# Windowed linear attention on one core: full out products of 144 columns with a selection behind them, k and v side by side, other orders at the ends

## The chip, the core and the metric

The kernel runs on one core of a Trainium2 chip, everything in fp32. The metric is the device time of one execution in microseconds, as a median over runs. TensorE (PE in the rows, its weight loads PEld) multiplies into PSUM; VectorE (DVE) and ScalarE (ACT) read PSUM; GpSimd (POOL) works in SBUF alone; SyncE (SP) issues the DMAs.

## The reference

`x` is 4 x 128 x 96 x 96. It is group-normalised (32 groups), cut into windows of 4 x 4 pixels and projected by a 1 x 1 convolution to q, k and v (16 heads of 8). A 5 x 5 average pool of q, k and v inside each window gives a second set of 16 heads. Each window and head gets linear attention, and both sets go through one more 1 x 1 convolution, a folded batch norm and the residual:

```
qkv = einsum('nchw,oc->nohw', xw, qkv_w); pooled = avg_pool5(qkv)
q, k, v = relu(msq[..., :8]), relu(msq[..., 8:16]), pad(msq[..., 16:], 1.0)
kv  = einsum('ngld,nglm->ngdm', k, v)
out = einsum('ngld,ngdm->nglm', q, kv)
out = out[..., :-1] / (out[..., -1:] + 1e-15)
y   = batch_norm(einsum('nchw,oc->nohw', out, proj_w));  return x + y
```

In a 4 x 4 window a 5 x 5 pool has only 9 different outputs, so the kernel carries 9 pooled pixels for each window and weights them.

## The kernel before

`x` is cut into 96 strips (`NS`) of 4 rows, 384 pixels or 24 windows each. All of `x` stays in SBUF (`x_all`). Each engine has its own instruction stream, written out by hand, and semaphores tie the streams together; nothing reorders them. TensorE's steps 1 to 94 are a hardware loop of two steps per pass; the other engines' streams are unrolled.

The names below end in `_f` or "full" for the 16 pixels of a window and in `_p` or "pooled" for the 9. TensorE's step `s` does, in this order:

- `conv_kv(s + 1)` (L587): k and v of the next strip, six products of 128 columns
- `transposes(s - 1)` (L695): the divided outputs turned back; waits for `kvc_f` of strip `s`
- `conv_kv_pooled(s + 1)` (L597)
- `project(s - 1)` (L704, L706): the output convolution; with `out_next` it first waits for `kvc_p` of strip `s`, since the out products that stand behind it need the masked tables
- `out_products(s)`, `out_products_pooled(s)` (L630): q times the table, 48 products of 72 columns each; the pooled ones wait for `added_f` and `y_copied`
- `kv_products(s + 1)` and its pooled twin (L615): k times v, 24 products of 144 columns and 16 of 216; the pooled ones write the PSUM banks 4 and 5 that the full out products also use, so they wait for `num_f`
- `conv_q(s + 1)` (L603, L604)

These products run as tiles of 64 rows x 32 columns of the array, eight in different places. A block of 32 rows holds two windows of 16 pixels. In a full out product of before each window of a block has its own product; its q stands in a `q_full` block padded with zeros for the other window, and the two accumulate in the same 72 columns.

VectorE's step `s`: `own_heads` for full and pooled (L509) copies the tables `kv` out of PSUM into `kvc_full` and `kvc_pool` with a mask, two instructions of 864 columns each, and gives `kvc_f` and `kvc_p`; then statistics of the next batch in some steps, `residual(s - 1)` (L515), and `divide` (L524, L525, L528) for full and pooled, which waits for `out_f` and `out_p`, reads PSUM and gives `num_f` and `num_p`.

ScalarE's step `s`: `relu_q`, `relu_q_pooled`, `relu_k`, `copy_v` of strip `s + 1`, `to_image` and `pooled_out` of strip `s - 1`, `relu_k_pooled`, then `masked_v_pooled`: six copies (L357, e = 0 to 5), with `copy_y_pooled` (L394) after the second. GpSimd normalises and pools the strip two ahead, then adds the pooled half of the residual. SP spreads `v_full` into `vm_full` by four DMAs a strip, loads later batches and stores.

Of the kernel before, what the change touches and what calls it, by code (L numbers as in the profile page):

```python
# [37 lines left out]
C_PACK = C_TP + EP  # L38
# [3 lines left out]
def constants():  # L42
# [14 lines left out]
    c[:, C_TP:C_TP + EP] = own_p * times  # L57
    pads = p % Q4 >= WP * PXP
# [4 lines left out]
def build(nc, x, wq, wkv, proj, bn, consts, out):  # L63
# [20 lines left out]
    with ExitStack() as ctx:  # L84
# [56 lines left out]
        KVF, OUTP, KVP, OUTF = 0, 2, 4, 4  # L141
        TRF, TRP = 0, 1
        Y_F, Y_P = 0, 1
        K_F, V_F = 2, 3
        K_P, V_P = 6, 7
        Q_F, Q_P = 6, 7
# [16 lines left out]
        projT_ready = sem("projT_ready")  # L163

        xn_ready, xp_ready = sem("xn_ready"), sem("xp_ready")
        k_f, v_f, k_p, v_p = sem("k_f"), sem("v_f"), sem("k_p"), sem("v_p")
# [8 lines left out]
        num_f, num_p = sem("num_f"), sem("num_p")  # L175
        tr_f, tr_p = sem("tr_f"), sem("tr_p")
# [17 lines left out]
        def over_strips(step):  # L194


            for s in range(NS):
                b, t = divmod(s - 3, SPB)
                at = t * 2 if s >= 3 and b + 1 < B and t < 2 * FOURS else None
                phase = t - 2 * FOURS if s >= 3 and b + 1 < B and 0 <= t - 2 * FOURS < 4 else None  # L200
                step(s, b + 1, at, phase)

# [50 lines left out]
        def _(pool):  # L253
            PL = 7
            pool.memset(xp[:], 0.0).then_inc(pads_zero, 1)
            pool.memset(q_full[:], 0.0).then_inc(pads_zero, 1)
# [7 lines left out]
            def normalise_and_pool(s, p):  # L264
# [11 lines left out]
                def link(ins, n):  # L276
                    ins.then_inc(pl, 1)
                    pool.wait_ge(pl, s * PL + n)
# [6 lines left out]
                rows = xd[:].rearrange("p (r g e c) -> p r g e c", r=WS, e=EF, c=WS)  # L285
                for r in range(WS):
# [10 lines left out]
                add(xo[:, :, :, 2, :], v3, h3[:, :, :, 3, :]).then_inc(pl, 1)  # L297
                add(xo[:, :, :, 1, :], xo[:, :, :, 0, :], h3[:, :, :, 3, :]).then_inc(xp_ready, 1)
# [23 lines left out]
            pool.wait_ge(pads_zero, 5)  # L322
            pool.wait_ge(dv_group, GS)
            normalise_and_pool(0, 0)
            normalise_and_pool(1, 1)
            over_strips(step)
            residual_pooled(NS - 1)

        @block.scalar
        def _(act):  # L330
            def relu_k(s):
                act.wait_ge(k_f, s + 1)
                wait(act, kv_f, s)
                act.activation(k_full[:].rearrange("p t c -> p (t c)"), ps[:, K_F, 0:TF * P],
                               ACT.Relu).then_inc(km_f, 1)

            def relu_k_pooled(s):
                act.wait_ge(k_p, s + 1)
                wait(act, kv_p, s)
                act.activation(k_pool[:].rearrange("p t c -> p (t c)"), ps[:, K_P, 0:TP * P],  # L340
                               ACT.Relu, scale=1 / 25.0).then_inc(km_p, 1)

            def copy_v(s):
                act.wait_ge(v_f, s + 1)
                wait(act, vm_f, 16 * EF * s)
                act.activation(v_full[:].rearrange("p t (h c) -> p t h c", c=HC)[:, :, :, 0:D],
                               ps[:, V_F, 0:TF * P].rearrange("p (t h m) -> p t h m", t=TF, m=D),
                               ACT.Copy).then_inc(v_copied, 1)

            def masked_v_pooled(s, between=None):  # L350

                act.wait_ge(v_p, s + 1)
                wait(act, kv_p, s)
                heads = vm_pool[:].rearrange("p e t (h c) -> p e t h c", c=HC)
                src = ps[:, V_P, 0:TP * P].rearrange("p (t h m) -> p t h m", t=TP, m=D)
                for e in range(EP):
                    last = act.activation(heads[:, e, :, :, 0:D], src, ACT.Copy, scale=col(C_VP + e))  # L357
                    if between is not None and e == 1:
                        copy_y_pooled(between)
                last.then_inc(vm_p, 1)  # L360

            def relu_q(s):


                act.wait_ge(q_f, s + 1)
                wait(act, out_f, s)
                act.activation(q_full[:].rearrange("p n e j -> p (n e) j").rearrange(  # L367
                                   "p (g w) j -> p g w j", w=EF)[:, :, :, 0:PX],
# [26 lines left out]

            def square_root(n):
# [6 lines left out]
            act.wait_ge(pads_zero, 5)  # L403

            def step(s, b, at, phase):
                relu_q(s)
                relu_q_pooled(s)
                if not is_last(s):
                    relu_k(s + 1)
                    copy_v(s + 1)  # L410
                if not is_first(s):
                    to_image(s - 1)
                    pooled_out(s - 1)
                if not is_last(s):
                    relu_k_pooled(s + 1)
                    masked_v_pooled(s + 1, None if is_first(s) else s - 1)
                elif not is_first(s):
                    copy_y_pooled(s - 1)
                if phase == 2:
                    square_root(b + 1)  # L420

            relu_k(0)
            copy_v(0)
            relu_k_pooled(0)
            masked_v_pooled(0)
            over_strips(step)
            to_image(NS - 1)
            pooled_out(NS - 1)
            copy_y_pooled(NS - 1)

        @block.vector
        def _(dve):
# [46 lines left out]

            dve.memset(mv[:], 0.0).then_inc(mv_zero, 1)  # L480
# [12 lines left out]
            group_rstd(0, 1)  # L493

# [22 lines left out]

            def divide(s, pooled):
                ready, done, turned, bank, tiles, den, o, step = (
                    (out_p, num_p, tr_p, OUTP, TP, den_pool, o_pool, 2) if pooled else  # L520
                    (out_f, num_f, tr_f, OUTF, TF, den_full, o_full, 0))
                dve.wait_ge(ready, s + 1)
                src = ps[:, bank:bank + G, 0:tiles * QG * KC].rearrange("p g (n c) -> p g n c", c=HC)
# [7 lines left out]
            def step(s, b, at, phase):  # L531
# [18 lines left out]
                elif phase == 3:  # L550
                    group_rstd(b, b + 2)
                if not is_first(s):
                    residual(s - 1)
                divide(s, False)
# [20 lines left out]
            residual(NS - 1)  # L575

        @block.tensor
        def _(pe):
            pe.wait_ge(loaded_w, 16 * 5)

            def conv_kv(s, p):
# [3 lines left out]
                for half, bank, done in ((0, K_F, k_f), (1, V_F, v_f)):  # L585
                    for t in range(TF):
                        last = pe.matmul(ps[:, bank, t * P:(t + 1) * P], xn[:, p, t * P:(t + 1) * P],  # L587
                                         wkv_sb[:, half * P:(half + 1) * P], start=True, stop=True)
                    last.then_inc(done, 1)

            def conv_kv_pooled(s, p):
# [3 lines left out]
                for half, bank, done in ((0, K_P, k_p), (1, V_P, v_p)):  # L595
                    for t in range(TP):
                        last = pe.matmul(ps[:, bank, t * P:(t + 1) * P], xp[:, p, t * P:(t + 1) * P],  # L597
# [176 lines left out]
```

## Time and profile before

| | |
|---|---|
| median of 3 runs | 895.9 us (895.72 to 898.23) |
| the profiled execution, its own time | 900.88 us |
| its span | 899.1 us |
| granted TensorE clock, mean | 0.993 |
| TensorE matmul busy | 859.1 us, 96% |
| VectorE / GpSimd / ScalarE busy | 77% / 74% / 57% |

The span runs from the first to the last instruction; the 1.8 us between it and the execution's own time lie around it. Busy shares are an average over the span. The engines' busy time doesn't say which of them the others wait for: that is read from the order of starts within a step.

### The profile page before, as it was taken

How to read it: one execution, taken by the hardware profiler on the slowest of the kernel's cores; microseconds unless marked ns; L12 is line 12 of the kernel's file. 1: busy time of each engine (PE TensorE's matmuls, PEld its weight loads, DVE VectorE, ACT ScalarE, POOL GpSimd, SP SyncE). 2: the span in 40 equal slices, each digit the busy share in tenths (PEclk: the TensorE clock that was granted, in tenths of full speed). 3: DMA queues.
4: the chain of work that ended last, by engine and by line, in shares of the span. 5: the costliest groups of instructions: out<-in, count | busy, mean ns of one | idle time of the engine just before them, and what ended most of it. 6: DMA issues, size and time to landing. Idle time of an engine off the chain costs nothing.

```text
span 899.1 us, 65691 instructions
## 1 busy us (share of the span) xinstructions
PE 859.1 (96%) x29282; PEld 740.6 (82%) x29282; DVE 695.4 (77%) x1236; ACT 509.9 (57%) x1350; POOL 666.7 (74%) x1641
## 2 busy tenths in 40 slices
PE   0789999999999999999999999999999999999996
PEld 0667888888888888888888888888888888888885
DVE  7466888888677888888776888888777777777775
ACT  0344656565655656565656556565656565565653
POOL 2666778777878777777878787777878787877772
PEclk9999999999999999999999999999999999999998
DMA  6122232111113232211113232211111111111111
GB/s 232 40 75 65 86 104 82 46 48 46 47 64 100 85 97 87 68 46 47 47 47 90 92 100 84 80 52 50 47 49 47 46 47 47 47 49 45 53 50 37
DMA packets 39082, 60.07 MB, mean 67 GB/s; under 512 B 8560, under 2 KB 33648, under 8 KB 39024
## 3 DMA queue, kind: packets, MB, share of 16 engines
q1 hardware_dynamic: 39024, 59.52, 19.7%
q14 instruction: 49, 0.40, 0.2%
q8 instruction: 9, 0.15, 0.1%
HBM read 19.38 MB, written 18.87 MB: 43 GB/s over the span
## 4 chain that ended last, share of the span: by engine, by line
PE 94%; DVE 2%; DMA 1%; issue 1%; SPq 0%; POOL 0%; ACT 0%; POOLq 0%; DVEq 0%
PE ps L630 23%; PE ps L615 17%; PE ps L587 15%; PE ps L597 9%; PE ps L603 9%; PE ps L704 7%; PE ps L695 6%; PE ps L706 4%; PE ps L604 4%; DVE stats L442 1%; DMA vm_full<-v_full 1%; DMA x_all<-x 1%; SPq L232 0%; DVE kvc_full L509 0%; POOL xn L287 0%
## 5 line engine op out<-in xcount | busy, mean ns | idle before, releaser
L357 ACT ACTIVATE vm_pool<-ps,cst 128x256 f32<-128x256 f32 x576 | 231.0, 481 | 5.1 <-PE ps L597 0.5
L367 ACT ACTIVATE q_full<-ps 128x384 f32<-128x384 f32 x96 | 47.3, 492 | 285.0 <-PE ps L603 285.0
L284 POOL TENSOR_TENSOR xd<-x_all,mean_t 128x384 f32<-128x384 f32 x96 | 79.5, 828 | 159.7 <-PE ps L604 143.0
L509 DVE TENSOR_TENSOR kvc_full<-ps,cst 128x864 f32<-128x864 f32 x192 | 193.2, 1048 | 5.2 <-PE ps L615 5.2
L509 DVE TENSOR_TENSOR kvc_pool<-ps,cst 128x864 f32<-128x864 f32 x192 | 193.1, 1047 | 1.4 <-PE ps L615 1.4
L587 PE MATMUL ps<-wkv_sb,xn 128*128 128x128 f32 x1152 | 146.4, 278 | 24.0 <-POOL xn L287 24.0
L587 PEld LDWEIGHTS ps<-wkv_sb,xn 128*128 128x128 f32 x1152 | 145.2, 194 | 24.0 <-issue 24.0
L262 POOL TENSOR_TENSOR x_all<-y_pool,x_all 128x96 f32<-128x96 f32 x384 | 150.8, 427 | 17.2 <-ACT y_pool L394 17.2
L287 POOL TENSOR_TENSOR xn<-xd,rstd_t 128x96 f32<-128x96 f32 x384 | 123.4, 369 | 7.5
L630 PEld LDWEIGHTS ps<-kvc_full,q_full 64*32 64x32 f32 x9216 | 108.0, 105 | 25.3 <-issue 25.2
L630 PE MATMUL ps<-kvc_full,q_full 64*32 64x72 f32 x9216 | 124.8, 230 | 0.0
L630 PE MATMUL ps<-kvc_pool,q_pool 64*32 64x72 f32 x9216 | 116.1, 231 | 2.9 <-issue 2.9
L515 DVE SCALAR_TENSOR_TENSOR x_all<-ps,shift,x_all 128x384 f32<-128x384 f32 x96 | 59.3, 618 | 71.2 <-PE ps L704 71.0
L630 PEld LDWEIGHTS ps<-kvc_pool,q_pool 64*32 64x32 f32 x9216 | 101.7, 105 | 3.7 <-issue 3.2
L597 PE MATMUL ps<-wkv_sb,xp 128*128 128x128 f32 x768 | 102.5, 277 | 0.7 <-POOL xp L262 0.7
L615 PE MATMUL ps<-vm_full,k_full 64*32 64x144 f32 x4608 | 95.6, 289 | 3.3 <-DMA vm_full<-v_full 3.3
L615 PE MATMUL ps<-vm_pool,k_pool 64*32 64x216 f32 x3072 | 96.0, 347 | 2.2 <-issue 2.2
L262 POOL TENSOR_TENSOR hs<-ht,xn 128x96 f32<-128x96 f32 x192 | 85.0, 443 | 15.0
L597 PEld LDWEIGHTS ps<-wkv_sb,xp 128*128 128x128 f32 x768 | 94.1, 193 | 1.0 <-POOL xp L262 1.0
L524 DVE TENSOR_SCALAR den_full<-ps 128x48 f32<-128x48 f32 x96 | 20.0, 208 | 92.2 <-PE ps L630 92.2
L603 PE MATMUL ps<-xn,wq_sb 128*128 128x384 f32 x192 | 88.8, 544 | 0.0
L704 PE MATMUL ps<-o_sb,projT 128*128 128x384 f32 x192 | 78.6, 491 | 0.7 <-ACT o_sb L382 0.7
(67 smaller groups left out, 1295.9 us busy)
## 6 DMA issues: line engine op xcount, KB each, us to landing
vm_full<-v_full SPq DMA_DIRECT2D x384, 54.0 KB, 1.9
out<-x_all SPq DMA_DIRECT2D x96, 192.0 KB, 1.9
x_all<-x SPq DMA_DIRECT2D x36, 384.0 KB, 3.5
x_all<-x SPq DMA_DIRECT2D x6, 768.0 KB, 8.1
cst<-consts SPq DMA_DIRECT2D x1, 170.0 KB, 11.0
wkv_sb<-wkv SPq DMA_DIRECT2D x1, 128.0 KB, 10.8
o_sb<-proj SPq DMA_DIRECT2D x1, 128.0 KB, 10.2
wq_sb<-wq SPq DMA_DIRECT2D x1, 64.0 KB, 10.5
```

The costliest lines, as they stand in the source:

```text
L262: return pool.tensor_tensor(o, a, b, ALU.add)
L284: link(pool.tensor_tensor(xd[:], x_all[:, s * SP:(s + 1) * SP], mean, ALU.subtract), 1)
L287: last = pool.tensor_tensor(xr[:, r], rows[:, r], rstd, ALU.mult)
L357: last = act.activation(heads[:, e, :, :, 0:D], src, ACT.Copy, scale=col(C_VP + e))
L509: last = dve.tensor_tensor(kvc[:, g], src.to_broadcast(shape), own, ALU.mult)
L515: dve.scalar_tensor_tensor(xs, ps[:, Y_F, 0:SP], shift[:], xs, ALU.add, ALU.add).then_inc(added_f, 1)
L587: last = pe.matmul(ps[:, bank, t * P:(t + 1) * P], xn[:, p, t * P:(t + 1) * P], wkv_sb[:, half * P:(half + 1) * P], start=True, stop=True)
L597: last = pe.matmul(ps[:, bank, t * P:(t + 1) * P], xp[:, p, t * P:(t + 1) * P], wkv_sb[:, half * P:(half + 1) * P], start=True, stop=True)
L603: pe.matmul(ps[:, Q_F, 0:SP], wq_sb[:], xn[:, p], start=True, stop=True).then_inc(q_f, 1)
L615: last = pe.matmul(ps[Q4 * i:Q4 * (i + 1), bank + r, t * n:(t + 1) * n], k[rows, t, Q4 * i:Q4 * (i + 1)], vm[rows, :, t, i * KC:(i + 1) * KC],
L630: last = pe.matmul(ps[Q4 * c:Q4 * (c + 1), bank + g, t * n:(t + 1) * n], blocks[rows, 4 * t + c, Q4 * e:Q4 * (e + 1)], kvc[rows, r, w], st ...
L704: pe.matmul(ps[:, Y_F, 0:SP], projT[:, 0:P], o_sb[:, 0:SP], start=True, stop=True).then_inc(y_f, 1)
```

## The change

Full out products: one product takes both windows of a block at once. Its stationary operand is the block's q without padding, its moving operand the tables of both windows, 144 columns, and it doesn't accumulate: 24 products in place of 48. Every row then has the results of both windows side by side, and only one is its own. `first_window` on ScalarE copies the results for window 0 of all rows to `sel_full` in SBUF (432 elements per partition); `copy_predicated` on VectorE then overwrites the rows of window 1. `divide` reads `sel_full`. Pooled out products stay as they were.

k and v: three (full) and two (pooled) products of 256 columns in place of six and four of 128, with one semaphore each (`conv_f`, `conv_p`). On ScalarE `copy_v` goes ahead of `relu_k`, and `relu_k` behind `pooled_out`. Strip 0 is normalised and pooled on VectorE; strip 1's k and v are made earlier; the last strip has another order and bank, and its pooled residual is VectorE's.

```diff
@@ bands and buffers
-        q_full = sb("q_full", [TF * 4, WF, Q4 + PX])
+        q_full = sb("q_full", [TF * 4, Q4])
+        sel_full = sb("sel_full", [G, TF, QG * KC])
-        K_F, V_F = 2, 3
-        K_P, V_P = 6, 7
-        Q_F, Q_P = 6, 7
+        KV_F, KV_P = 2, 6
+        Q_F, Q_P = 7, 6
@@ ScalarE
+            def first_window(s):
+                act.wait_ge(out_f, s + 1)
+                wait(act, num_f, s)
+                bank = OUTF_LAST if is_last(s) else OUTF
+                act.activation(sel_full[:], full_windows(bank)[:, :, :, 0], ACT.Copy).then_inc(win_f, 1)
...
                 for e in range(EP):
                     last = act.activation(heads[:, e, :, :, 0:D], src, ACT.Copy, scale=col(C_VP + e))
                     if between is not None and e == 1:
                         copy_y_pooled(between)
+                    if e == 3 and s > 0:
+                        first_window(s - 1)
@@ VectorE, divide, full
-                dve.wait_ge(ready, s + 1)
-                src = ps[:, bank:bank + G, 0:tiles * QG * KC].rearrange("p g (n c) -> p g n c", c=HC)
+                    dve.wait_ge(win_f, s + 1)
+                    own = col(C_WIN + 1).bitcast(mybir.dt.uint32).unsqueeze(2).unsqueeze(3)
+                    dve.copy_predicated(sel_full[:], own.to_broadcast([P, G, TF, QG * KC]),
+                                        full_windows(bank)[:, :, :, 1]).then_inc(sel_f, 1)
+                    dve.wait_ge(sel_f, s + 1)
+                    src = sel_full[:].rearrange("p g t (n c) -> p g (t n) c", c=HC)
@@ TensorE
+            def out_group_f(t, bank):
+                n = WF * QG * KC
                 for g in range(G):
                     rows = slice(H64 * g, H64 * (g + 1))
                     for c in range(4):
-                        r, w = c // QG, t * QG * wins + c % QG * wins + e
-                        last = pe.matmul(ps[Q4 * c:Q4 * (c + 1), bank + g, t * n:(t + 1) * n],
-                                         blocks[rows, 4 * t + c, Q4 * e:Q4 * (e + 1)], kvc[rows, r, w],
-                                         start=e == 0, stop=e == wins - 1)
+                        r, w = c // QG, (t * QG + c % QG) * WF
+                        last = pe.matmul(ps[Q4 * c:Q4 * (c + 1), bank + g, t * n:(t + 1) * n],
+                                         q_full[rows, 4 * t + c], kvc_full[rows, r, w:w + WF],
+                                         start=True, stop=True)
@@ kv_products_pooled
-                wait(pe, num_f, s)
+                wait(pe, sel_f, s)
```

VectorE, one step in the loop's steady part, before (each group ends with the tables of the next step; the word behind "waits" is the semaphore):

```order
L524 TENSOR_SCALAR den_full<-ps 128x48 [waits out_f]
L525 RECIPROCAL den_full<-den_full 128x48 [waits dv]
L528 TENSOR_TENSOR o_full<-ps,den_full 128x2x192 [waits tr_f,dv]
L524 TENSOR_SCALAR den_pool<-ps 128x32 [waits out_p]
L525 RECIPROCAL den_pool<-den_pool 128x32 [waits dv]
L528 TENSOR_TENSOR o_pool<-ps,den_pool 128x2x128 [waits tr_p,dv]
L509 TENSOR_TENSOR kvc_full<-ps,cst 128x864 [waits out_f,kv_f]
```

The same place after the change:

```order
L613 COPY_PREDICATED sel_full<-cst,ps 128x432 [waits win_f]
L617 TENSOR_SCALAR den_full<-sel_full 128x48 [waits sel_f]
L618 RECIPROCAL den_full<-den_full 128x48 [waits dv]
L621 TENSOR_TENSOR o_full<-sel_full,den_full 128x2x192 [waits tr_f,dv]
L617 TENSOR_SCALAR den_pool<-ps 128x32 [waits out_p]
L618 RECIPROCAL den_pool<-den_pool 128x32 [waits dv]
L621 TENSOR_TENSOR o_pool<-ps,den_pool 128x2x128 [waits tr_p,dv]
L577 TENSOR_TENSOR kvc_full<-ps,cst 128x864 [waits out_f,kv_f]
```

One instruction is new, and the first wait of the group is now for ScalarE's `win_f` and not for TensorE's `out_f`.

ScalarE, the same step, before:

```order
L340 ACTIVATE k_pool<-ps 128x256 [waits kv_p,k_p]
L357 ACTIVATE vm_pool<-ps,cst 128x32x8 [waits kv_p,v_p]
L357 ACTIVATE vm_pool<-ps,cst 128x32x8
L394 ACTIVATE y_pool<-ps 128x216 [waits y_done,y_p]
L357 ACTIVATE vm_pool<-ps,cst 128x32x8 x4
```

And after:

```order
L351 ACTIVATE k_full<-ps 128x384 [waits kv_f,conv_f]
L356 ACTIVATE k_pool<-ps 128x256 [waits kv_p,conv_p]
L373 ACTIVATE vm_pool<-ps,cst 128x32x8 [waits kv_p,conv_p]
L373 ACTIVATE vm_pool<-ps,cst 128x32x8
L411 ACTIVATE y_pool<-ps 128x216 [waits y_done,y_p]
L373 ACTIVATE vm_pool<-ps,cst 128x32x8 x2
L418 ACTIVATE sel_full<-ps 128x432 [waits num_f,out_f]
L373 ACTIVATE vm_pool<-ps,cst 128x32x8 x2
```

The window copy stands behind the fourth of the six `vm_pool` copies, and `k_full` has moved to the front of this piece.

## Rows read from the trace of the kernel before

**Rows 1.** The page: busy time by engine, and the chain that ended last.

```profile
PE 859.1 (96%) x29282; PEld 740.6 (82%) x29282; DVE 695.4 (77%) x1236; ACT 509.9 (57%) x1350; POOL 666.7 (74%) x1641
...
PE 94%; DVE 2%; DMA 1%; issue 1%; SPq 0%; POOL 0%; ACT 0%; POOLq 0%; DVEq 0%
```

**Rows 2.** Timeline of PE in one step: start us, length us, instruction, count.

```profile
234.38 0.81 PE L704 MATMUL ps<-o_sb,projT 128*128 128x384 f32 x2
235.02 0.53 PE L706 MATMUL ps<-o_sb,projT 128*128 128x216 f32 x2
235.48 1.30 PE L630 MATMUL ps<-kvc_full,q_full 64*32 64x72 f32 x96
236.57 1.20 PE L630 MATMUL ps<-kvc_pool,q_pool 64*32 64x72 f32 x96
237.66 0.98 PE L615 MATMUL ps<-vm_full,k_full 64*32 64x144 f32 x48
238.39 0.98 PE L615 MATMUL ps<-vm_pool,k_pool 64*32 64x216 f32 x32
...
240.41 1.50 PE L587 MATMUL ps<-wkv_sb,xn 128*128 128x128 f32 x12
241.75 0.49 PE L695 MATMUL ps<-cst,o_full 128*128 128x128 f32 x3
...
243.19 0.81 PE L704 MATMUL ps<-o_sb,projT 128*128 128x384 f32 x2
```

**Rows 3.** Timeline of DVE in the same step.

```profile
236.82 0.21 DVE L524 TENSOR_SCALAR den_full<-ps 128x48 f32<-128x48 f32 x1 [0.97 <-PE ps L630]
...
238.02 0.18 DVE L524 TENSOR_SCALAR den_pool<-ps 128x32 f32<-128x32 f32 x1
...
238.97 2.01 DVE L509 TENSOR_TENSOR kvc_full<-ps,cst 128x864 f32<-128x864 f32 x2
240.90 2.01 DVE L509 TENSOR_TENSOR kvc_pool<-ps,cst 128x864 f32<-128x864 f32 x2
```

**Rows 4.** Timeline of ACT in the same step.

```profile
235.59 0.35 ACT L394 ACTIVATE y_pool<-ps 128x216 f32<-128x216 f32 x1 [0.17 <-PE ps L706]
235.84 1.57 ACT L357 ACTIVATE vm_pool<-ps,cst 128x256 f32<-128x256 f32 x4
```

**Rows 5.** Timeline near the end, where PE does wait for other engines.

```profile
883.50 2.01 DVE L509 TENSOR_TENSOR kvc_full<-ps,cst 128x864 f32<-128x864 f32 x2
...
885.57 0.55 PE L695 MATMUL ps<-cst,o_full 128*128 128x128 f32 x3 [0.42 <-DVE kvc_full L509]
...
886.69 0.91 PE L704 MATMUL ps<-o_sb,projT 128*128 128x384 f32 x2 [0.36 <-ACT o_sb L382]
...
888.01 0.35 ACT L394 ACTIVATE y_pool<-ps 128x216 f32<-128x216 f32 x1 [1.12 <-PE ps L706]
```

**Rows 6.** Groups by line and shape: busy us, mean ns of one.

```profile
L509 DVE TENSOR_TENSOR kvc_full<-ps,cst 128x864 f32<-128x864 f32 x192 | 193.2, 1048 | 5.2 <-PE ps L615 5.2
L262 POOL TENSOR_TENSOR x_all<-y_pool,x_all 128x96 f32<-128x96 f32 x384 | 150.8, 427 | 17.2 <-ACT y_pool L394 17.2
...
L528 DVE TENSOR_TENSOR o_full<-ps,den_full 128x384 f32<-128x384 f32 x96 | 53.6, 559 | 3.3
...
L367 ACT ACTIVATE q_full<-ps 128x384 f32<-128x384 f32 x96 | 47.3, 492 | 285.0 <-PE ps L603 285.0
...
L375 ACT ACTIVATE q_pool<-ps 128x216 f32<-128x216 f32 x96 | 34.5, 360 | 0.2 <-PE ps L604 0.2
```

**Rows 7.** Timeline of PE in the first steps.

```profile
27.62 2.08 PE L597 MATMUL ps<-wkv_sb,xp 128*128 128x128 f32 x8 [0.72 <-POOL xp L262]
...
43.14 1.69 PE L615 MATMUL ps<-vm_full,k_full 64*32 64x144 f32 x48 [2.06 <-DMA vm_full<-v_full]
...
50.13 0.81 PE L704 MATMUL ps<-o_sb,projT 128*128 128x384 f32 x2
...
68.93 0.96 PE L615 MATMUL ps<-vm_pool,k_pool 64*32 64x216 f32 x30 [2.18 <-issue]
```

More of the change, by code:

```diff
@@ L37 @@
 C_TP = C_VP + EP
-C_PACK = C_TP + EP
+C_WIN = C_TP + EP
+C_PACK = C_WIN + WP
 N_CONST = C_PACK + P
@@ L407, in step @@
                 relu_q_pooled(s)
-                if not is_last(s):
-                    relu_k(s + 1)
+                if not is_first(s) and not is_last(s):
                     copy_v(s + 1)
@@ L413, in step @@
                     pooled_out(s - 1)
+                if not is_first(s) and not is_last(s):
+                    relu_k(s + 1)
                 if not is_last(s):
@@ L416, in step @@
                     masked_v_pooled(s + 1, None if is_first(s) else s - 1)
-                elif not is_first(s):
+                else:
                     copy_y_pooled(s - 1)
+                    first_window(s)
                 if phase == 2:
                     square_root(b + 1)
+            copy_v(0)
             relu_k(0)
-            copy_v(0)
             relu_k_pooled(0)
             masked_v_pooled(0)
+            copy_v(1)
+            relu_k(1)
             over_strips(step)
@@ L516, in residual, with residual_pooled_last @@
                                          ALU.add).then_inc(added_f, 1)
+            def residual_pooled_last():
+                s = NS - 1
+                dve.wait_ge(y_p, s + 1)
+                dve.wait_ge(added_f, s + 1)
+                dve.wait_ge(y_done, s)
+                src = ps[:, Y_P, 0:SPP].rearrange("p (w r c) -> p w r c", r=NP, c=NP)
+                dst = x_all[:, s * SP:(s + 1) * SP].rearrange("p (r w c) -> p w r c", r=WS, c=WS)
+                ends, ends_p, mid, mid_p = slice(0, WS, WS - 1), slice(0, NP, NP - 1), slice(1, 3), slice(1, 2)
+                for rows, rows_p in ((ends, ends_p), (mid, mid_p)):
+                    for cols, cols_p in ((ends, ends_p), (mid, mid_p)):
+                        part = dst[:, :, rows, cols]
+                        last = dve.tensor_tensor(part, src[:, :, rows_p, cols_p].to_broadcast([P, NW, 2, 2]), part,
+                                                 ALU.add)
+                last.then_inc(y_done, 1)
             def divide(s, pooled):
@@ L584, in conv_kv @@
                 wait(pe, num_p, s - 1)
[L585 to L589, printed above, removed]
+                for t in range(TF):
+                    bank, at = KV_F + t // 2, t % 2 * 2 * P
+                    last = pe.matmul(ps[:, bank, at:at + 2 * P], xn[:, p, t * P:(t + 1) * P], wkv_sb[:],
+                                     start=True, stop=True)
+                last.then_inc(conv_f, 1)
             def conv_kv_pooled(s, p):
@@ L594, in conv_kv_pooled @@
                 wait(pe, qm_p, s)
-                for half, bank, done in ((0, K_P, k_p), (1, V_P, v_p)):
-                    for t in range(TP):
-                        last = pe.matmul(ps[:, bank, t * P:(t + 1) * P], xp[:, p, t * P:(t + 1) * P],
-                                         wkv_sb[:, half * P:(half + 1) * P], start=True, stop=True)
-                    last.then_inc(done, 1)
+                for t in range(TP):
+                    last = pe.matmul(ps[:, KV_P, t * 2 * P:(t + 1) * 2 * P], xp[:, p, t * P:(t + 1) * P], wkv_sb[:],
+                                     start=True, stop=True)
+                last.then_inc(conv_p, 1)
             def conv_q(s, p):
@@ L618, in kv_tile @@
                 return last
-            def out_tile(pooled, t, e):
-                q, kvc, bank, wins = (q_pool, kvc_pool, OUTP, WP) if pooled else (q_full, kvc_full, OUTF, WF)
-                n = QG * KC
-                blocks = q[:].rearrange("p n e j -> p n (e j)")
+            def out_group_f(t, bank):
+                n = WF * QG * KC
                 for g in range(G):
@@ L654, in out_wait @@
                     pe.wait_ge(qm_p, s + 1)
-                pe.wait_ge(kvc_p, s + 1)
+                    pe.wait_ge(kvc_f, s + 1)
+                else:
+                    pe.wait_ge(kvc_p, s + 1)
             def out_products(s):
@@ L663, in out_products @@
                 for t in range(TF):
-                    for e in range(WF):
-                        last = out_tile(False, t, e)
+                    last = out_group_f(t, OUTF_LAST if is_last(s) else OUTF)
                 last.then_inc(out_f, 1)
```

129 lines of the change are left out of this document (102 added, 27 removed).

## The prediction

> **What bounds the kernel now.** I read the page first, then the timelines of TensorE, VectorE and ScalarE side by side over one step in the steady part, then the two ends. The page says TensorE: its matmuls are busy 96% of the span and the chain that ended last runs 94% through it [rows 1]. In the step no matmul group starts late; from one `project` to the next, 234.38 to 243.19, is 8.81 us [rows 2]. So a shorter TensorE stream would pay, as long as nobody else becomes late.
>
> The page can't say how close the next one is. For that I follow VectorE from the end of the full out products. `den_full` starts at 236.82, 2.44 us after `project`; VectorE then never pauses until both `own_heads` are done: den_full at 236.82, den_pool at 238.02, kvc_full at 238.97, kvc_pool at 240.90 and 2.01 us long, so `kvc_p` comes at 242.91 [rows 3]. The next `project` waits for `kvc_p` and starts at 243.19 [rows 2]. A wait from VectorE to TensorE takes 0.05 to 0.06 us (kvc_full ends at 885.51, the matmul starts at 885.57 [rows 5]). The ring project, out products, divide, tables, project has thus 0.28 - 0.05 = 0.23 us of slack in 8.81. That is the number on which everything below rests: two engines take turns in this ring, and work put into it costs its full time beyond 0.23 us and beyond what TensorE's own part of it gives back.
>
> **What the change takes from TensorE.** The full out products take 236.57 - 235.48 = 1.09 us [rows 2]. The new ones have shape, count and tile places of the full kv products: 24 of 64x32 with 144 columns, which take 238.39 - 237.66 = 0.73 us [rows 2]. Saving 0.36 us a step. k and v side by side: two instructions of 384 columns take 0.64 us (234.38 to 235.02), 0.83 ns a column, so a product of 256 columns costs 2 x 0.215 = 0.43 us; three make 1.29 us where the twelve instructions of 128 columns now take 1.34 (240.41 to 241.75) [rows 2]. With the pooled ones that is some 0.08 us a step. Alone, TensorE's stream would need 8.81 - 0.44 = 8.37 us.
>
> **What it puts into the ring.** I walk once round it, from the start of `project` (0).
>
> 1. To `copy_y_pooled`. Now 235.59 - 234.38 = 1.21 us [rows 2, 4]. That is for a TensorE that didn't wait, and so had its weights loaded ahead. Where it did wait before `project`, it took 888.01 - 886.69 = 1.32 us [rows 5]. I take 1.32, since it will wait.
> 2. To the window copy. Behind the copy of y (0.25 us to the next start) stand the copies e = 2 and e = 3. Four of these take 1.57 us, the last 0.48 of it, so they start 0.36 apart [rows 4]; in all 0.97 us, and `first_window` could start at 2.29. Its own wait, `out_f`: the out products start 0.11 + 1.10 = 1.21 us after `project` and end some 0.98 later (the kv products' length [rows 2]), at 2.19 + 0.04. So ScalarE's order decides, by 0.06 us only; without the copies ahead of it the window would start hardly sooner.
> 3. The window copy, 432 elements from PSUM. ScalarE takes 492 ns for 384 and 360 ns for 216 [rows 6], 0.79 ns an element: 0.53 us, and 0.04 to wake VectorE. 2.86.
> 4. `copy_predicated`, 432 elements. The trace has none. From the rows of VectorE that read PSUM, 559 ns for 384 and 1048 for 864 [rows 6], 1.02 ns an element: 0.61 us and 0.03 to the next. It can't be under 0.45 (the elements at the rate of those rows, no fixed part), and if it read its output as well, at two passes, it would be near 1.06. I take 0.61, since it moves one tensor from PSUM to SBUF as they do. 3.50.
> 5. The full divide, as now, 238.02 - 236.82 = 1.20; the pooled one to `own_heads`, 238.97 - 238.02 = 0.95; the tables 242.91 - 238.97 = 3.94 [rows 3]; 0.05 to TensorE. 9.64.
>
> The ring becomes 9.64 us against TensorE's 8.37, and 0.83 more than the 8.81 of now. The saving of 0.36 is inside that number: the out products end earlier, and then two copies in a row, 1.2 us, stand where nothing stood.
>
> Do other waits inside the step add to it? Counted from `project`: `sel_f` comes at 3.5 and the pooled kv products are due at 1.21 + 0.73 + 1.09 + 0.73 = 3.76; the last `vm_pool` copy, pushed back by the window, ends near 3.6: no stall. `num_p` comes at about 5.6, when `conv_kv` is due at 5.8: none. `kvc_f` comes at 5.65 + 2.01 = 7.66 and `transposes` were due at 7.1, so they wait 0.6 us; they and the pooled convolution take 243.19 - 241.75 = 1.44 [rows 2] and end at 9.2, inside the ring's 9.64. `relu_k` moved behind `pooled_out` makes ScalarE's y copy ready by some 0.2 us still. These cost nothing as long as VectorE is behind by more.
>
> **The sum.** 93 periods from the first `project` to the last in the loop: 93 x 0.83 = +77 us. First steps: the pooled part of strip 0 no longer stands ahead of strip 1 on GpSimd (TensorE waited for it until 27.62), and strip 1's v is spread early, which spares the 2.06 us wait at 43.14 before the `project` at 50.13 [rows 7]; with the earlier tables of strip 0 I take -4.5 (bounds -2 and -6). First pass of the loop: TensorE stood in stretches like the 2.18 us ahead of 68.93 for nothing that the profile shows [rows 7]; with idle time of over 1 us a step part of them is covered and the stream is shorter: -4 (0 to -7). Last strip: it gets a window copy and a selection and loses the step through GpSimd, about 0. Sum +69 us. The profiled execution took 900.88 us for its span of 899.1, so its like would be near 970; the median of the runs shown is 5 us lower, and I add the 69 to that: **965 us**.
>
> **Rivals.**
>
> *TensorE stays the bound* (faster). For it: [rows 1], and that both copies run on engines that idle 23 and 43% of the time. It holds if what is put between `out_f` and `den_full` stays under 0.23 + 0.36 - 0.11, about 0.5 us; from there the ring decides. Window copy and selection are priced at 1.2. If I have a wait wrong and the ring isn't closed, the period is 8.37: 93 x -0.44 = -41, with the first steps' -8: 847 us. Chance 6%.
>
> *It doesn't do what it says, or cancels.* The selection would have to cost almost nothing, or the masks run while TensorE still multiplies: no change within what a measurement tells (0.3%). 2%, and 1% for a slightly faster one.
>
> *VectorE's new operands collide with GpSimd* (slower still). `divide` reads `sel_full` and `den_full`, both in SBUF, where it read one from PSUM. If such an instruction had to wait for the one that GpSimd has under way, 427 ns long with GpSimd busy 74% [rows 1, 6], it would cost up to 0.3 us a step in the ring: +28, 993 us. No instruction in VectorE's steady part now has that form, so the trace doesn't speak. Chance 10%. The Trainium skill says this of the two (Advanced Engine Details and Errata, GPSIMD Details): GpSimd "shares a read and a write interface with DVE (conflicts with DVE instructions in a 2-port perf mode or with two SBUF inputs)"; by that rule this rival would be the forecast and the sum 993, but the page gives no size and no run here shows one yet.
>
> *The selection takes two passes*, 1.06 us: +0.45 x 93 = +42, 1007 us. 6%.
>
> The forecast itself, the ring at 9.4 to 9.9 us: 75%.
>
> **Range.** The ends come from the ring: 9.45 us (restart at 1.21 and copies at their lower bounds) and -11 in the first steps together give 944; the collision gives 993. 944 to 994 holds the forecast and most of the collision. Faster 7%, same 2%, slower 91%.
>
> **What would show it.** Starts of `project` 9.6 us apart in the steady part; matmul busy down; TensorE idle ahead of `transposes` (about 0.6 us, for kvc_full) and ahead of `project` (0.4, for kvc_pool); full out products 0.73 us; window copy 0.53 and selection 0.61 us, one right behind the other; VectorE idle only ahead of residual and selection. Wrong it would be if `project` starts 8.4 us apart with no wait for kvc_pool ahead of it, if the selection or the divide has another length than in steps 4 and 5, or if a wait for `xn` or the spread v turns up instead.

## The result and the profile after

The changed kernel takes **981.1 us** (980.34 to 981.4, four runs) where the one before takes 895.9 (895.72 to 898.23): ratio 1.094, 95% interval 1.092 to 1.096. It is slower, as forecast, by 16 us more than the 965 predicted and inside the range of 944 to 994. Its profiled execution has a span of 979.1 us, 80.0 more than before.

Its page (against [rows 1]), busy time by engine, then the chain that ended last:

```profile
PE 878.8 (90%) x23714; PEld 650.1 (66%) x23714; DVE 769.7 (79%) x1348; ACT 546.1 (56%) x1445; POOL 659.6 (67%) x1623
...
DVE 63%; PE 14%; ACT 13%; issue 8%; DMA 1%; DVEq 0%; SPq 0%; ACTq 0%
```

The chain has moved from 94% TensorE to 63% VectorE, 14% TensorE and 13% ScalarE: a ring through three engines. VectorE is only 79% busy in it. No engine is full; the order of their turns is what takes the time. Matmul busy time rose from 859.1 to 878.8 us although 5,568 matmuls are gone, so that line alone would mislead. e2 below, with the same products and the ring's copies taken out, has 827.2.

TensorE over one step, from one `project` to the next (against [rows 2]; the bracket is idle time before the row and what ended it):

```profile
408.33 0.88 PE L822 MATMUL ps<-o_sb,projT 128*128 128x384 f32 x2 [0.39 <-DVE kvc_pool L577]
409.06 0.53 PE L824 MATMUL ps<-o_sb,projT 128*128 128x216 f32 x2
409.51 0.99 PE L725 MATMUL ps<-kvc_full,q_full 64*32 64x144 f32 x48
410.27 1.25 PE L739 MATMUL ps<-kvc_pool,q_pool 64*32 64x72 f32 x96
411.42 0.98 PE L712 MATMUL ps<-vm_full,k_full 64*32 64x144 f32 x48
...
416.13 0.55 PE L813 MATMUL ps<-cst,o_full 128*128 128x128 f32 x3 [0.30 <-DVE kvc_full L577]
...
418.15 0.88 PE L822 MATMUL ps<-o_sb,projT 128*128 128x384 f32 x2 [0.39 <-DVE kvc_pool L577]
```

VectorE in the same step (against [rows 3]):

```profile
411.16 0.66 DVE L613 COPY_PREDICATED sel_full<-cst,ps 128x432 f32<-128x432 uint32 x1 [1.28 <-ACT sel_full L418]
411.85 0.27 DVE L617 TENSOR_SCALAR den_full<-sel_full 128x48 f32<-128x48 f32 x1
412.15 0.45 DVE L618 RECIPROCAL den_full<-den_full 128x48 f32<-128x48 f32 x1
412.64 0.56 DVE L621 TENSOR_TENSOR o_full<-sel_full,den_full 128x384 f32<-128x384 f32 x1
413.12 0.18 DVE L617 TENSOR_SCALAR den_pool<-ps 128x32 f32<-128x32 f32 x1
...
414.06 2.01 DVE L577 TENSOR_TENSOR kvc_full<-ps,cst 128x864 f32<-128x864 f32 x2
415.99 2.01 DVE L577 TENSOR_TENSOR kvc_pool<-ps,cst 128x864 f32<-128x864 f32 x2
```

ScalarE there (against [rows 4]):

```profile
409.62 0.35 ACT L411 ACTIVATE y_pool<-ps 128x216 f32<-128x216 f32 x1 [0.52 <-PE ps L824]
409.87 0.83 ACT L373 ACTIVATE vm_pool<-ps,cst 128x256 f32<-128x256 f32 x2
410.59 0.54 ACT L418 ACTIVATE sel_full<-ps 128x432 f32<-128x432 f32 x1
```

GpSimd there adds the pooled half of the residual. It ends at 412.05, beside `den_full` and ahead of `o_full`, and then rests until 414.42:

```profile
410.49 1.56 POOL L271 TENSOR_TENSOR x_all<-y_pool,x_all 128x96 f32<-128x96 f32 x4
```

Follow it as one chain. TensorE starts `project` (408.33) when `kvc_pool` is there; ScalarE copies y (409.62), two masked v copies, then the window (410.59); VectorE, idle for 1.28 us, selects (411.16), divides (411.85 to 414.06) and masks both tables, done at 418.00; TensorE starts `project` again at 418.15. This round is 9.82 us. From the first `project` (44.86) to the last in the loop (958.56) it is 913.70 us for 93 rounds, 9.82 in the mean; before, the steady round was 8.81.

### The profile page after: what moved, and what is told of

It is laid out like the page before. It is cut to its first block, busy times and chain, and to the rows that moved or that the text cites. A ratio compares the mean times of both kernels' runs of the same rounds, so it can differ in the third digit from the quotient of the medians.

```text
span 979.1 us, 54842 instructions
## 1 busy us (share of the span) xinstructions
PE 878.8 (90%) x23714; PEld 650.1 (66%) x23714; DVE 769.7 (79%) x1348; ACT 546.1 (56%) x1445; POOL 659.6 (67%) x1623
## 4 chain that ended last, share of the span: by engine, by line
DVE 63%; PE 14%; ACT 13%; issue 8%; DMA 1%; DVEq 0%; SPq 0%; ACTq 0%
DVE kvc_full L577 19%; DVE kvc_pool L577 18%; PE ps L822 9%; ACT vm_pool L373 8%; DVE sel_full L613 6%; DVE o_full L621 5%; DVE den_full L618 4%; ACT sel_full L418 4%; PE ps L824 4%; DVE den_pool L618 3%; DVE den_full L617 3%; DVE stats L469 1%; DVE den_pool L617 1%; PE ps L712 0%; DMA x_all<-x 0%
## 5 line engine op out<-in xcount | busy, mean ns | idle before, releaser
L373 ACT ACTIVATE vm_pool<-ps,cst 128x256 f32<-128x256 f32 x576 | 240.8, 477 | 0.0
L684 PE MATMUL ps<-wkv_sb,xn 128*128 128x256 f32 x576 | 147.9, 393 | 24.0 <-DVE xn L533 23.1
L613 DVE COPY_PREDICATED sel_full<-cst,ps 128x432 f32<-128x432 uint32 x96 | 63.3, 659 | 120.0 <-ACT sel_full L418 120.0
L684 PEld LDWEIGHTS ps<-wkv_sb,xn 128*128 128x128 f32 x576 | 102.6, 191 | 56.6 <-issue 46.1
L822 PE MATMUL ps<-o_sb,projT 128*128 128x384 f32 x192 | 85.5, 527 | 35.8 <-DVE kvc_pool L577 35.8
L739 PEld LDWEIGHTS ps<-kvc_pool,q_pool 64*32 64x32 f32 x9216 | 114.0, 105 | 5.2 <-issue 5.2
L362 ACT ACTIVATE v_full<-ps 128x384 f32<-128x384 f32 x96 | 47.4, 493 | 103.1 <-PE ps L684 103.1
L693 PE MATMUL ps<-wkv_sb,xp 128*128 128x256 f32 x384 | 99.6, 382 | 0.7 <-ACT q_pool L392 0.6
L725 PE MATMUL ps<-kvc_full,q_full 64*32 64x144 f32 x4608 | 95.1, 287 | 0.6 <-DVE kvc_pool L577 0.6
L725 PEld LDWEIGHTS ps<-kvc_full,q_full 64*32 64x32 f32 x4608 | 66.8, 106 | 26.0 <-issue 26.0
```

Source lines behind the costliest of these rows:

```text
L613: dve.copy_predicated(sel_full[:], own.to_broadcast([P, G, TF, QG * KC]), full_windows(bank)[:, :, :, 1]).then_inc(sel_f, 1)
L684: last = pe.matmul(ps[:, bank, at:at + 2 * P], xn[:, p, t * P:(t + 1) * P], wkv_sb[:], start=True, stop=True)
L693: last = pe.matmul(ps[:, KV_P, t * 2 * P:(t + 1) * 2 * P], xp[:, p, t * P:(t + 1) * P], wkv_sb[:], start=True, stop=True)
L725: last = pe.matmul(ps[Q4 * c:Q4 * (c + 1), bank + g, t * n:(t + 1) * n], q_full[rows, 4 * t + c], kvc_full[rows, r, w:w + WF], start=True, ...
L739: last = pe.matmul(ps[Q4 * c:Q4 * (c + 1), OUTP + g, t * n:(t + 1) * n], blocks[rows, 4 * t + c, Q4 * e:Q4 * (e + 1)], kvc_pool[rows, r, w ...
L822: pe.matmul(ps[:, Y_F, 0:SP], projT[:, 0:P], o_sb[:, 0:SP], start=True, stop=True).then_inc(y_f, 1)
```

## The experiments

All are compared with runs of the kernel before on the same chip, whose median was 896.5 us in both groups (e1 to e4, e5 to e8). The "period" is the distance of two `project`s in the steady part.

**e1_old_out: the changed kernel without its out products, selection and window copy.** k and v side by side, ScalarE's order and both ends stay.

```diff
-                    if e == 3 and s > 0:
-                        first_window(s - 1)
@@ VectorE divide, full
-                    dve.wait_ge(win_f, s + 1)
-                    dve.copy_predicated(sel_full[:], ...)
+                dve.wait_ge(ready, s + 1)
+                src = ps[:, bank:bank + G, ...]
@@ TensorE
-                n = WF * QG * KC
+                n = QG * KC
+                for e in range(WF):
+                    ... start=e == 0, stop=e == WF - 1
```

> The changed kernel with only its full out products put back: 48 products of 72 columns from zero-padded q blocks, no window copy, no selection, divide reads PSUM; k and v side by side, ScalarE's new order and both ends stay changed. Ring theory (window copy and selection stand in the ring project, out products, divide, tables): the ring falls back to about 8.6 us, TensorE's own stream of about 8.75 us decides, no wait for kvc_pool ahead of project; 93 x -0.08, -5 for the first strips and 0 to -7 for the first pass of the loop against before: 876 to 885 us, so faster than before. Rival (the side-by-side products with their one semaphore, or ScalarE's new order, are what is late): it stays above 950 us.

Measured 888.6 us (886.47 to 889.07), ratio 0.989 (0.986 to 0.993): **the one version here that does the whole computation in less time than before**. That gain is 0.9%. The period is 8.76, and `den_full` reads PSUM again and takes 208 ns. The time is 3.6 us above the top of the 876 to 885 that I expected: the first `project` comes at 48.80, 1.3 us sooner than before and not 5. The whole loss of the change, and more, sits in the out products and what they need behind them.

**e2_no_copies: no window copy and no selection.** The divide reads window 0's columns for all rows.

```diff
-                        first_window(s - 1)
-                    dve.copy_predicated(sel_full[:], ...)
+                src = ps[:, bank:bank + G, 0:tiles * QG * KC]
```

> The changed kernel without window copy and selection: divide reads half of the full out products' columns straight from PSUM, so the results of rows are mixed up and the output isn't the reference's. Ring theory: the ring loses 0.57 (window copy) and 0.69 us (selection) and about 0.07 of den_full, and is at 8.45 to 8.5 us beside TensorE's 8.4; 981 - 93 x 1.33 = 857 us (850 to 868). Rival (TensorE's new forms or the wait for SBUF ports are the cost): above 900 us.

Measured 862.4 us (861.81 to 863.93), ratio 0.961 (0.958 to 0.964). With nothing put into the ring the change saves 34 us, and the 119 us between this and 981.1 are the price of the two copies. Nothing in the ring holds TensorE here. Its timeline, then the four DMAs by which SyncE spreads v for the full kv products (L705):

```profile
405.13 1.03 PE L686 MATMUL ps<-wkv_sb,xp 128*128 128x256 f32 x4
405.99 0.81 PE L815 MATMUL ps<-o_sb,projT 128*128 128x384 f32 x2
406.64 0.53 PE L817 MATMUL ps<-o_sb,projT 128*128 128x216 f32 x2
407.10 0.99 PE L718 MATMUL ps<-kvc_full,q_full 64*32 64x144 f32 x48
407.85 1.25 PE L732 MATMUL ps<-kvc_pool,q_pool 64*32 64x72 f32 x96
409.10 0.98 PE L705 MATMUL ps<-vm_full,k_full 64*32 64x144 f32 x48
```

```profile
405.30 2.38 SPq L242 DMA_DIRECT2D vm_full<-v_full  x4
```

`project` starts right behind the pooled convolution, with no idle time. The period is 8.57, where the prediction gave TensorE alone 8.37. The full out products do fall from 1.09 to 0.75 us, start to start; but from the start of the pooled ones behind them, which were not edited, to the kv products it is now 1.25 in place of 1.09. Both together take 409.10 - 407.10 = 2.00 us against 2.18 [rows 2], a saving of 0.18 and not 0.36.

Some 0.10 of that 1.25 isn't the products' own. In the changed kernel the same pooled products, behind the same full ones, take 411.42 - 410.27 = 1.15. In e2 the kv products start 2.02 us behind the issue of the fourth DMA (median of the steady steps), in the changed kernel 3.07, and there that DMA has landed 1.88 us after its issue. So the kv products of e2 very likely wait for the spread v. The trace of e2 has no landing times, so this is inferred and not shown. Without that wait the saving is 2.18 - 1.91 = 0.27, as the changed kernel's rows have it, and TensorE's own stream is near 8.57 - 0.10 = 8.47 us, an estimate from these rows.

**e3_no_window: no window copy on ScalarE.** The selection stays and waits for the out products; rows of window 0 keep an old value.

```diff
-                        first_window(s - 1)
-                    dve.wait_ge(win_f, s + 1)
+                    dve.wait_ge(ready, s + 1)
```

> The changed kernel without ScalarE's window copy alone; the selection waits for the out products themselves and the rows of window 0 keep old numbers, so the output isn't the reference's. Ring theory: the selection starts at the end of the out products, 2.23 us after project and not 2.83, period 9.82 - 0.60 = 9.22 us, time 981 - 56 = 925 us (920 to 930). Rival (ScalarE's copy is hidden and only VectorE's added busy time counts, 0.69 us a step): no change, 981.

Measured 940.3 us (939.4 to 940.77), ratio 1.048 (1.044 to 1.051), 15 more than expected. The window copy is so worth 41 us, less than its 0.57 us in the ring (53 us), because something else grew. One stretch of VectorE:

```profile
403.14 0.65 DVE L611 COPY_PREDICATED sel_full<-cst,ps 128x432 f32<-128x432 uint32 x1
403.82 0.42 DVE L615 TENSOR_SCALAR den_full<-sel_full 128x48 f32<-128x48 f32 x1
```

`den_full`, 128 x 48 elements, takes 203/418/512 ns (least, median, most over 96), twice what it takes from PSUM. `o_full` grows too: 559/584/670, where it is 557/558/564 in e1. The selection comes sooner here, and both now fall beside GpSimd's additions, which end at 404.93:

```profile
403.36 1.57 POOL L272 TENSOR_TENSOR x_all<-y_pool,x_all 128x96 f32<-128x96 f32 x4
```

In the mean `den_full` is 402 ns against 274 in the changed kernel and `o_full` 588 against 562: 0.15 us a step, 14 us over 93 rounds, the miss of 15. That is the collision that e6 then tries by itself.

**e4_kv_only: the kernel before, with only k and v side by side.** ScalarE's order stays that of before.

```diff
-                for half, bank, done in ((0, K_F, k_f), (1, V_F, v_f)):
-                    for t in range(TF):
-                        last = pe.matmul(ps[:, bank, ...], xn[...], wkv_sb[:, half * P:(half + 1) * P], ...)
-                    last.then_inc(done, 1)
+                for t in range(TF):
+                    last = pe.matmul(ps[:, bank, at:at + 2 * P], xn[...], wkv_sb[:], ...)
+                last.then_inc(conv_f, 1)
```

> The kernel before with k and v side by side alone (products of 256 columns, one semaphore, banks as in the changed kernel; ScalarE's order as before). Ring theory: the ring has no part in this; TensorE 0.04 to 0.08 us shorter a step: 888 to 893 us. Rival (one semaphore makes ScalarE late and it becomes the bound): slower than 900.

A miss: 914.6 us (913.81 to 915.3), ratio 1.019 (1.015 to 1.022), slower where I expected 888 to 893. The rival written down beside it, one semaphore that makes ScalarE late, comes nearer to it. ScalarE, then TensorE in the same step:

```profile
407.82 0.50 ACT L338 ACTIVATE k_full<-ps 128x384 f32<-128x384 f32 x1 [0.92 <-PE ps L590]
408.21 0.49 ACT L349 ACTIVATE v_full<-ps 128x384 f32<-128x384 f32 x1
408.58 0.50 ACT L385 ACTIVATE o_sb<-ps 128x384 f32<-128x384 f32 x1
408.95 0.37 ACT L392 ACTIVATE o_sb<-ps 128x216 f32<-128x216 f32 x1
```

```profile
406.32 1.46 PE L590 MATMUL ps<-wkv_sb,xn 128*128 128x256 f32 x6
...
409.13 0.91 PE L706 MATMUL ps<-o_sb,projT 128*128 128x384 f32 x2
```

With one semaphore for k and v, `relu_k` can start only when all three products are done, at 407.82, 1.50 us after the first of them starts (406.32). Behind it stand `copy_v` and both `o_sb` copies, on which `project` now waits. The view of waits has it in every step (us in total, times, longest):

```profile
PEld ps L706 <- ACT o_sb L385: 32.6, 96, 0.6
```

The period is 8.97, 0.21 more than in e1, and 0.19 of it stand here: `project` starts 409.13 - 408.16 = 0.97 us after the pooled convolution and lasts 1.20, with its weights loaded late; in e1 it is 0.86 and 1.12.

The change's other ScalarE order (`relu_k` behind `pooled_out`) takes one 0.4 us copy out from ahead of `o_sb`. e1 has it, and its period is 8.76. (e1 also has the change's two ends, which the period leaves out.) In the changed kernel the point is hidden by the ring, but the side-by-side products and the new order belong together.

**e5_window_early: the window copy right behind the y copy**, ahead of the third and fourth `vm_pool` copy. It tests the rival that ScalarE's queue holds the window back.

```diff
-                    if e == 3 and s > 0:
+                    if e == 1 and s > 0:
```

> The changed kernel with the window copy right behind the copy of y, ahead of the third and fourth vm_pool copy instead of behind them. Ring theory: the window copy then waits for the out products themselves, which end 2.23 us after project; now it starts at 2.26 (410.59 - 408.33), so 0.03 us a step at most: 977 to 982 us, no change that can be told. Rival (ScalarE's queue is what delays the window copy): 0.7 us a step off, near 915.

Measured 989.5 us (986.7 to 990.22), ratio 1.103 (1.100 to 1.107): 8 us slower than the changed kernel, where no change was expected (977 to 982), and not the 915 of the rival. ScalarE:

```profile
569.26 0.35 ACT L411 ACTIVATE y_pool<-ps 128x216 f32<-128x216 f32 x1 [0.52 <-PE ps L824]
570.22 0.53 ACT L418 ACTIVATE sel_full<-ps 128x432 f32<-128x432 f32 x1 [0.61 <-PE ps L725]
```

With nothing ahead of it, the window copy idles for 0.61 us until the out products are done, and starts 570.22 - 567.97 = 2.25 us after `project`; in the changed kernel it is 410.59 - 408.33 = 2.26. The two copies in front of it were free. What got worse is `den_full`, 202/325/537 ns against 202/261/487, in the mean 343 against 274. The last four `vm_pool` copies are now late, and the pooled kv products wait for them:

```profile
572.36 0.97 PE L712 MATMUL ps<-vm_pool,k_pool 64*32 64x216 f32 x32 [0.33 <-ACT vm_pool L373]
```

That wait doesn't reach the ring: the tables start 573.75 - 572.80 = 0.95 us after `den_pool`, as before [rows 3]. The steady round is 9.89 against 9.83 in the mean, and `den_full` is 0.07 of it: all of what the period lost. The profiled execution is 5 us longer than the changed kernel's; the median lies 3 us above it, and no trace shows those 3.

**e6_no_pool_residual: GpSimd's pooled residual cut to one element.** The pooled half of the residual is left out. It tests whether GpSimd lengthens `den_full`.

```diff
-                        last = add(part, src[:, :, rows_p, cols_p].to_broadcast([P, NW, 2, 2]), part)
+                last = add(x_all[:, s * SP:s * SP + 1], y_pool[:, 0:1], ...)
```

> The changed kernel with GpSimd's four residual additions a strip cut to one of a single element, so the pooled half is missing from the output; GpSimd is idle while VectorE runs selection and full divide. In the changed kernel the addition that makes den_full takes 274 ns from SBUF on the mean, between 202 and 487, where it took 208 from PSUM. Collision theory (it waits for GpSimd's access to SBUF): 205 to 215 ns in nearly every strip, ring 0.06 us shorter, 973 to 977 us. Rival (reading SBUF costs that much by itself): stays at 260 to 275 ns, 980.

Measured 973.2 us (972.1 to 973.59), ratio 1.084 (1.081 to 1.087), as expected. VectorE:

```profile
408.07 0.66 DVE L611 COPY_PREDICATED sel_full<-cst,ps 128x432 f32<-128x432 uint32 x1 [1.28 <-ACT sel_full L416]
408.76 0.20 DVE L615 TENSOR_SCALAR den_full<-sel_full 128x48 f32<-128x48 f32 x1
409.00 0.45 DVE L616 RECIPROCAL den_full<-den_full 128x48 f32<-128x48 f32 x1
409.49 0.56 DVE L619 TENSOR_TENSOR o_full<-sel_full,den_full 128x384 f32<-128x384 f32 x1
```

`den_full` is 201/203/227 ns and the period 9.74. So the collision is real; it costs 0.07 us a step in the changed kernel, in all 8 of the 85 us. The other 77 stay without it.

**e7_project_later: the full out products ahead of `project`**, the window copy ahead of the y copy, the residual between selection and divide. If the ring is the cause, taking `project` out of it must help.

```diff
-                    project(s - 1, out_next=True)
+                    out_wait(s)
                 out_products(s)
+                    project(s - 1)
@@ VectorE
+                select(s)
                     residual(s - 1)
```

> The changed kernel with the full out products ahead of project on TensorE, the window copy ahead of the copy of y on ScalarE, and the residual between selection and divide on VectorE; the same work in another order. Ring theory: project leaves the ring. From the end of kvc_pool: 0.15 + 0.98 to the end of the out products, 0.04 + 0.57 window copy, 0.69 selection, 0.65 residual, 1.27 and 0.94 divides, 3.94 tables: 9.23 us a step; 981 - 93 x 0.59 = 926 us, up to 940 if den_full meets GpSimd more often. Rival (VectorE's added work as such is the bound, in whatever order, or TensorE pays for another change of tile form): 965 or more.

Measured 962.0 us (960.7 to 962.57), ratio 1.072 (1.069 to 1.075): 19 us better than the changed kernel, so the direction holds; the size is well short of the 926 to 940 that I expected, and 962 is nearer to the rival's 965 or more. TensorE, VectorE, GpSimd:

```profile
563.64 1.02 PE L697 MATMUL ps<-wkv_sb,xp 128*128 128x256 f32 x4
564.60 0.99 PE L729 MATMUL ps<-kvc_full,q_full 64*32 64x144 f32 x48
565.52 0.91 PE L826 MATMUL ps<-o_sb,projT 128*128 128x384 f32 x2
...
567.55 1.21 PE L743 MATMUL ps<-kvc_pool,q_pool 64*32 64x72 f32 x96 [0.75 <-DVE x_all L583]
```

```profile
562.08 2.01 DVE L577 TENSOR_TENSOR kvc_pool<-ps,cst 128x864 f32<-128x864 f32 x2
...
566.27 0.64 DVE L606 COPY_PREDICATED sel_full<-cst,ps 128x432 f32<-128x432 uint32 x1 [1.26 <-ACT sel_full L418]
566.81 0.60 DVE L583 SCALAR_TENSOR_TENSOR x_all<-ps,shift,x_all 128x384 f32<-128x384 f32 x1
...
568.20 0.56 DVE L624 TENSOR_TENSOR o_full<-sel_full,den_full 128x384 f32<-128x384 f32 x1
```

```profile
567.90 1.90 POOL L271 TENSOR_TENSOR x_all<-y_pool,x_all 128x96 f32<-128x96 f32 x4
```

`kvc_pool` ends at 564.09 but the out products start at 564.60: TensorE isn't ready. Its stream was pushed back by 0.75 us, because the pooled out products use the bank of `project`'s result and wait until the residual, now behind the selection, has read it. Another ring had formed: out products, window, selection, residual, pooled out products, kv products, convolutions, out products, 9.60 us long. I had seen only the first. GpSimd's row has the collision from its other side: its four additions stand beside `o_full` and take 1.90 us, where they take 1.56 in the changed kernel.

**e8_select_twice: the selection done twice.** It prices one instruction in the ring.

```diff
+                    dve.copy_predicated(sel_full[:], ...).then_inc(sel_1, 1)
+                    dve.wait_ge(sel_1, s + 1)
                     dve.copy_predicated(sel_full[:], ...).then_inc(sel_f, 1)
```

> The changed kernel with the selection done twice in a row, the same result. Ring theory: every microsecond of the selection is in the ring, 0.69 us more a step: 981 + 64 = 1045 us (1040 to 1050). Rival (part of the selection is covered by idle time of VectorE, which waits 1.3 us ahead of it in each step): under 1020.

Measured 1041.0 us (1040.46 to 1041.37), ratio 1.160 (1.157 to 1.164), as expected.

```profile
403.00 0.66 DVE L613 COPY_PREDICATED sel_full<-cst,ps 128x432 f32<-128x432 uint32 x1 [1.28 <-ACT sel_full L418]
403.69 0.65 DVE L616 COPY_PREDICATED sel_full<-cst,ps 128x432 f32<-128x432 uint32 x1
404.37 0.20 DVE L620 TENSOR_SCALAR den_full<-sel_full 128x48 f32<-128x48 f32 x1
```

A second selection, 0.69 us from start to start, adds 59.9 us over 96 strips, 0.62 us each. It would be 0.69, but `den_full`, 0.68 later than in the changed kernel, falls beside GpSimd's work less often and has a median of 203 ns in place of 261. So nearly all of what stands on this path arrives in the end.

## Why the prediction was right, step by step

The mechanism is the predicted one: the ring closes over `kvc_pool` and `project`, and what is put into it costs its full time. e2, e3, e7 and e8 show it from four sides: take both copies out, 119 us, and the ring no longer holds TensorE; take one out, 41 us; move `project` out, 19 us; add a selection, 60 us. The walk, piece by piece, as predicted and as the rows above have it:

| piece | predicted | measured |
|---|---|---|
| `project` to the y copy | 1.32 | 1.29 |
| to the window copy | 0.97 | 0.97 |
| window copy and wake | 0.57 | 0.57 |
| selection | 0.64 | 0.69 |
| full divide | 1.20 | 1.27 |
| pooled divide | 0.95 | 0.94 |
| tables | 3.94 | 3.94 |
| `kvc_p` to `project` | 0.05 | 0.15 |
| sum | 9.64 | 9.82 |

- **Selection.** One pass over 432 elements and not two: 659 ns in the mean. Of the bounds, 0.45 and 1.06, the rate of the PSUM readers was the right one to take; it was 0.05 low.
- **Full divide.** `den_full` takes 274 ns in the mean where it took 208. The rival of the operands that collide with GpSimd was right in kind and too dear, up to 0.3 us a step where 0.07 came. Here only the denominator pays. `o_full` now has two SBUF inputs and takes 562 ns against 559 [rows 6], but that is no test: GpSimd's additions are over before it starts, and in 93 of the 96 steps nothing runs on GpSimd beside it. Where they do meet, one of the two gets longer: `o_full` itself in e3 (median 584 ns, up to 670), in e7 mostly GpSimd's additions (up to 761 ns for one, where e1, whose `o_full` reads PSUM, has at most 455). The reciprocal, from SBUF to SBUF, keeps 453 ns in e3 and e7 too, with GpSimd busy beside it. The Trainium skill (Advanced Engine Details and Errata, GPSIMD Details) speaks of "DVE instructions in a 2-port perf mode or with two SBUF inputs": for `o_full` e3 and e7 agree. The same page (2x-2p Requirements, Instruction Support) lets a copy or a tensor_scalar with source and destination in SBUF run in such a mode, which fits the denominator; no run here shows the mode itself.
- **Wake of TensorE.** I took 0.05 from a wait ahead of the transposes [rows 5]; there the changed kernel has 0.06 to 0.07 too (`kvc_full` ends at 416.07, the matmul starts at 416.13). Ahead of `project` it is 0.15: `kvc_pool` ends at 418.00, the matmul starts at 418.15. The view of line 770, where TensorE waits for `kvc_p`, has part of the reason:

```profile
L770 PEldq EVENT_SEMAPHORE  x94: 51/51/51, 44.8 to 958.5; - x94
```

This wait is an instruction of its own on TensorE's sequencer, 51 ns long, once a step. In e7 the pooled out products start 0.14 after the residual that they wait for (567.41, 567.55). What the other 0.1 us is made of stays open. The kernel before has the same 51 ns instruction in the same place (its L656, 94 times), so its slack was nearer to 0.28 - 0.15 = 0.13 us and not the predicted 0.23.
- **What TensorE gives back.** The full out products alone do give some 0.33 us, but the unedited pooled ones behind take 1.15 in place of 1.09: together 1.91 against 2.18, a saving of 0.27 and not 0.36. With no copies in the ring the period is 8.57 us (e2), not 8.37: 0.09 of the 0.20 is this, and 0.10 is very likely the wait for the spread v, which the prediction left out. It made no difference to the forecast, since the ring decides; it would have spoilt the rival "TensorE stays the bound" by 19 us, 866 and not 847 (e2 measured 862.4).
- **k and v side by side.** Harmless in the ring, and a gain only together with ScalarE's new order (e4 against e1). I took it as a saving of 0.08 us a step without asking what its single semaphore delays.
- **The ends.** The first `project` starts at 44.86 and not 50.13: -5.3, predicted -4.5. The first two rounds of the loop take 9.74 and 9.84, no more than the others, where before they took 10.63 and 14.59 against 8.83: -7.6, predicted -4. The forecast that idle time covers what TensorE loses there holds: it still stands for 0.84 us ahead of 48.65 and 1.10 ahead of 58.67 with nothing that the profile shows as the reason, and the round is no longer for it. In e1, with TensorE as the bound, they take 10.94 and 11.01. The last strip: 979.1 - 958.56 = 20.5 us from the last `project` in the loop to the end, against 899.1 - 878.84 = 20.3.
- **Sum.** Before, the rounds took (878.84 - 50.13 - 7.6) / 93 = 8.829 us in the mean, now 9.825. 93 x 0.996 = +92.6, -5.3, -7.6 and +0.3 make +80.0, the difference of the spans. The forecast of +69 is short by 93 x 0.18 = 17 in the ring, of which the mean round of before, 0.02 above the one that I read, takes 2 back, and the ends another 4: 11 us. The rest of the 16 us is where the sum started from: 970 was lowered by 5 to the median of before, whose profiled execution was a long one, but the changed kernel's profiled execution has almost its median.
- **The signs.** `project` starts 9.82 us apart where 9.6 was written; the idle 0.39 ahead of it with `kvc_pool` as the releaser, and the two copies one right behind the other, came as written. Two were off. "Matmul busy down" did not come (859.1 to 878.8), and the idle time ahead of `transposes` is 0.30 in the row and not 0.6.

Not settled: why the first rounds of the loop lose time at all, and why matmul busy rose.

## What to carry to other kernels

When two engines take turns in a closed ring, write down its slack first (here 0.13 of 8.81 us, with the wait ahead of `project` at its measured 0.15): a change that saves on one and puts a handover and two copies between them pays only for what is under that slack, however idle the engines are that do the copies. Before merging results under one semaphore, look who stands behind the consumer on its engine. And when a step is taken out of one ring, look for the next ring that closes through it (e7).

## What the runs showed of the hardware

- A short VectorE instruction from SBUF to SBUF (`tensor_scalar`, 128 x 48) takes 202 to 537 ns beside a working GpSimd (e3, e5, after) and 201 to 227 with GpSimd's pooled residual gone (e6); from PSUM it takes 207 to 209 (e1). Moving it by 0.7 us within the step brings its median from 261 to 203 (e8).
- Where a VectorE instruction with two SBUF inputs (`tensor_tensor`, 128 x 384) meets a GpSimd addition whose operands are in SBUF, one of the two gets longer: the first takes 559/584/670 ns in e3, one of the second up to 761 in e7. Beside a quiet GpSimd the first takes 558/559/581 (e8), and with one input in PSUM 557/558/564 beside a busy one (e1). A reciprocal of 128 x 48 from SBUF to SBUF takes 452 to 457 in every run.
- The 48 pooled out products of 72 columns take 1.09 us behind full products of 72 columns [rows 2] and 1.15 behind full products of 144 in the same tiles (the changed kernel).
- TensorE's wait for `kvc_p` is an instruction of its own and lasts 51 ns (L770 of the changed kernel); from the releaser's end to the first matmul it is 0.15 us there, and 0.06 ahead of the transposes.
